# Layer-0 pair products of a DLRM tower (CIN) made for three tiles at once

## The reference, cut to what matters

```
prev = x
for k in range(3):
    z = einsum('bmd,bhd->bdmh', x, prev).reshape(b, 16, m * h)
    t = einsum('bdc,co->bdo', z, ws[k]) + bs[k]      # ws[0]: 39*39 x 128, ws[1], ws[2]: 128*39 x 128
    t = transpose(t, (0, 2, 1))
    t = t / sqrt(sum(t * t, axis=(-2, -1)))          # one norm per example
    logit.append(t); prev = t
features = sum(concatenate(logit, axis=1), axis=-1)  # then a small 400-512-256-1 network
```

## Time and profile before

| | |
|---|---|
| median of three runs | 1061.17 us |
| the profiled execution | 1062.48 us |
| its span, first to last instruction | 1060.8 us |
| TensorE (PE) busy | 97% |
| VectorE (DVE) busy | 93% |
| GpSimd (POOL) busy | 82% |
| ScalarE (ACT) busy | 75% |
| granted TensorE clock | 1.000 of full speed in the mean |

### The profile page before, as it was taken

How to read it: one execution, slowest core, us unless ns; L and a number is a source line. 1 busy time by engine, 2 the same in 40 slices (tenths; PEclk the granted TensorE clock), 3 DMA queues, 4 the chain that set the end, 5 groups by cost and what they waited for, 6 DMA issues and landing times.

```text
span 1060.8 us, 17970 instructions
## 1 busy us (share of the span) xinstructions
PE 1028.2 (97%) x4320; PEld 782.4 (74%) x4320; DVE 983.6 (93%) x3344; ACT 791.3 (75%) x2655; POOL 865.9 (82%) x729
## 2 busy tenths in 40 slices
PE   2999999999999999999999999999999999999998
PEld 0477777878777787877778787777878777788884
DVE  2589999999999999999999999999999999999993
ACT  3476877868788786868778687777868778788872
POOL 6777988889898888988888898888889888577770
PEclk9999999999999999999999999999999999999999
DMA  5650030302303030120303012030301203000000
GB/s 188 129 143 12 3 88 3 89 2 52 96 4 88 3 87 4 21 71 2 89 3 87 5 28 64 3 89 2 85 7 17 74 3 89 1 1 1 2 1 1
DMA packets 75892, 46.10 MB, mean 43 GB/s; under 512 B 55689, under 2 KB 58633, under 8 KB 75658
## 3 DMA queue, kind: packets, MB, share of 16 engines
q1 hardware_dynamic: 68487, 38.59, 15.2%
q10 hardware_dynamic: 2179, 5.07, 1.4%
q0 software_dynamic: 5120, 1.29, 1.4%
HBM read 42.99 MB, written 1.94 MB: 42 GB/s over the span
## 4 chain that ended last, share of the span: by engine, by line
PE 48%; POOL 19%; DVE 18%; issue 9%; ACT 5%; DMA 1%; POOLq 0%; DVEq 0%; SPq 0%; ACTq 0%
POOL sums L432 14%; DVE sums L946 12%; PE acc L778 8%; PE bank_d L722 7%; PE bank_d L723 6%; PE bank_d L724 6%; PE bank_a L724 6%; PE bank_a L722 6%; PE bank_a L723 6%; POOL gathered L415 5%; ACT scaled L560 4%; DVE bank_d L946 2%; DVE sums L965 1%; ACT sums L560 1%; PE turned L799 1%
## 5 line engine op out<-in xcount | busy, mean ns | idle before, releaser
L432 POOL TENSOR_TENSOR sums<-sums,scaled 128x512 f32<-128x512 f32 (+1 forms) x512 | 645.1, 1262 | 133.4 <-ACT scaled L560 97.4
L946 DVE SCALAR_TENSOR_TENSOR sums<-bank_d,x_col,sums 128x128 f32<-128x128 f32 x2304 | 654.2, 339 | 29.3 <-PE bank_d L724 20.2
L560 ACT ACTIVATE scaled<-bank_a,x_col 128x128 f32<-128x128 f32 x1920 | 551.5, 385 | 139.8 <-PE bank_a L724 132.7
L722 PE MATMUL bank_d<-w_hi,prev_lo 128*128 128x512 f32 x640 | 288.0, 450 | 6.2 <-DVE sums L965 4.7
L722 PE MATMUL bank_a<-w_hi,prev_lo 128*128 128x512 f32 (+1 forms) x640 | 263.9, 412 | 2.6 <-issue 1.3
L724 PE MATMUL bank_d<-w_hi,prev_hi 128*128 128x512 f32 x640 | 252.5, 394 | 0.0
L723 PE MATMUL bank_d<-w_lo,prev_hi 128*128 128x512 f32 x640 | 252.1, 394 | 0.0
L724 PE MATMUL bank_a<-w_hi,prev_hi 128*128 128x512 f32 (+1 forms) x640 | 245.3, 383 | 0.0
L723 PE MATMUL bank_a<-w_lo,prev_hi 128*128 128x512 f32 (+1 forms) x640 | 245.1, 383 | 0.0
L560 ACT ACTIVATE sums<-bank_a,x_col 128x128 f32<-128x128 f32 x512 | 146.1, 369 | 76.8 <-PE bank_a L724 75.9
L415 POOL DMA_INDIRECT gathered<-in_table,idx x160 | 177.2, 1108 | 28.5 <-issue 18.3
(11 more groups left out here) (84 smaller groups left out, 528.2 us busy)
## 6 DMA issues: line engine op xcount, KB each, us to landing
x_pairs<-x_scratch SPq DMA_DIRECT2D x135, 156.0 KB
x_pairs<-x_scratch SPq DMA_DIRECT2D x96, 78.0 KB
gathered<-in_table,idx POOLq DMA_INDIRECT x160
x_sq<-x_scratch SPq DMA_DIRECT2D x32, 64.0 KB
x_pairs<-x_scratch SPq DMA_DIRECT2D x92, 22.0 KB
x_scratch<-gathered SPq DMA_DIRECT2D x16, 72.0 KB
w_raw<-in_w ACTq DMA_DIRECT2D x1, 1024.0 KB, 5.1
w_raw<-in_w ACTq DMA_DIRECT2D x1, 896.0 KB
```

The source lines that it names most:

```text
L432: nc.gpsimd.tensor_tensor(out=sums[:, n % SUMS, 0:w, :], in0=sums[:, n % SUMS, 0:w, :], in1=scaled[:, a - 1, 0:w, :], op=ALU.add).then_inc ...
L560: op = nc.scalar.activation(to[:, i, :], bank_a[at % A_RING][:, i * UNITS:(i + 1) * UNITS], ACT.Copy, scale=x_of(c, q, a * PER_BANK + i))
L722: nc.tensor.matmul(to, lo, w_h, start=True, stop=False)
L946: nc.vector.scalar_tensor_tensor(out=taken(n, u) if u in LEFT else total, in0=taken(n, u), scalar=x_of(c, q, A_FIELDS + u), in1=total, op0 ...
```

## The change

The groups become [0, 1, 2], [3, 4, 5] and [6]. The extra pairs move from tiles 0, 1, 2, 3 to tiles 0, 1, 3, 4, so that each group has one copy of `x_rep`; the third tile of a group gets a third load into partitions 117 to 127 whose products meet no weights (its matmul has 117 rows). The products of a chunk then come after field 8 of the last step of the iteration before, after field 8 of step 1 and after field 2 of step 2. The matmuls of tiles 0 to 2 go to places 1, 4 and 7 of step 0, tile 3 to place 9 of step 1, tiles 4 and 5 to places 1 and 3 of step 2, and the squares stay at place 8 of step 2. `turn_x` moves to field 9 of step 2. Chunk 0 is made tile by tile throughout, with a semaphore of its own for the tiles within a group.

```diff
--- before.py
+++ after.py
@@ -27,10 +27,11 @@
 PAIR_TILES = len(PAIR_OFFSETS) // PER_TILE
 PAIR_ROWS = PER_TILE * FIELDS
 EXTRA = 128 - PAIR_ROWS
-EXTRA_PAIRS = [(0, 0, 1, FIELDS - 1), (2, 2 * EXTRA, 2 * EXTRA + 1, 2 * EXTRA - 1)]
+EXTRA_PAIRS = [(0, 0, 1, FIELDS - 1), (3, 2 * EXTRA, 2 * EXTRA + 1, 2 * EXTRA - 1)]
 SQUARES = PAIR_TILES
-PAIR_GROUPS = [[0, 1], [2, 3], [4, 5], [6]]
+PAIR_GROUPS = [[0, 1, 2], [3, 4, 5], [6]]
 NP = len(PAIR_GROUPS)
+WITH_EXTRA = [first + n for first, _, *partners in EXTRA_PAIRS for n in range(len(partners))]
 
 PICKED = 3
 SCRATCH_FIELDS = FIELDS + 5 * SLOT_FIELDS
@@ -124,11 +125,15 @@
         _made = []
         _summed = {(0, 0): [0, 1], (0, 2): [2, 3], (0, 4): [4, 5], (0, 6): [6]}
     else:
-        _first = (step_at(_it, 0), 2) if _it == 1 else (step_at(_it - 1, 7), 12)
-        _made = [_first, (step_at(_it, 0), 12), (step_at(_it, 1), 12 if _it > 1 else 17), (step_at(_it, 2), 5)]
-        _summed = {(step_at(_it, 0), 5): [0], (step_at(_it, 0), 8): [1], (step_at(_it, 1), 1): [2],
-                   (step_at(_it, 1), 4): [3], (step_at(_it, 2), 1): [4], (step_at(_it, 2), 4): [5],
-                   (step_at(_it, 2), 8): [6]}
+        _i = [step_at(_it, q) for q in range(3)]
+        if _it == 1:
+            _made = [(_i[0], 2), (_i[1], 4), (_i[2], 2)]
+            _summed = {(_i[0], 5): [0], (_i[0], 7): [1], (_i[0], 9): [2]}
+        else:
+            _last = step_at(_it - 1, 7)
+            _made = [(_last, 8), (_i[1], 8), (_i[2], 2)]
+            _summed = {(_i[0], 1): [0], (_i[0], 4): [1], (_i[0], 7): [2]}
+        _summed.update({(_i[1], 9): [3], (_i[2], 1): [4], (_i[2], 3): [5], (_i[2], 8): [6]})
     if _it:
         SQUARES_AT[step_at(_it, 1), 3] = _c
     PAIRS_AT.update({at: (_c, p) for p, at in enumerate(_made)})
@@ -138,7 +143,7 @@
 
 SQ = 32
 OVER = FIELDS - SQ
-TURNS_AT = {((0, 12) if _c == 1 else (step_at(_c - 1, 1), 8)): _c for _c in range(1, CHUNKS)}
+TURNS_AT = {((0, 12) if _c == 1 else (step_at(_c - 1, 2), 9)): _c for _c in range(1, CHUNKS)}
 
 
 W_LOADS = {1: [(0, 16), (16, 28), (28, 39)], 2: [(0, 14), (14, 27), (27, 39)]}
@@ -277,6 +282,7 @@
         turns_made = sem("turns_made")
         picked = sem("picked")
         pairs_made = sem("pairs_made")
+        first_pairs_made = sem("first_pairs_made")
         pairs_summed = sem("pairs_summed")
         x_sq_loaded = sem("x_sq_loaded")
         x_col_made = sem("x_col_made")
@@ -316,9 +322,11 @@
         y_done = sem("y_done")
         y_stored = sem("y_stored")
 
-        PAIR_LOADS = [2 * PER_TILE + 3, 2 * PER_TILE + 3, PER_TILE, 0]
-
-        NOT_LOADED = [PER_TILE + 2, 1, 0, 0]
+        PAIR_LOADS = [2 * PER_TILE + 4, 2 * PER_TILE + 4, 0]
+
+        NOT_LOADED = [PER_TILE + 3, 0, 0]
+
+        FIRST_SINGLY = [i for tiles in PAIR_GROUPS for i in tiles[:-1]]
         R_STEPS = 4
         TOP_LOADS = 2 * 3 + 2
 
@@ -358,11 +366,11 @@
                 for kk in range(PER_TILE):
                     load_rows(queue, c, p, x_rot[kk * FIELDS:(kk + 1) * FIELDS, tiles[0]:tiles[0] + len(tiles), :],
                               PAIR_OFFSETS[PER_TILE * tiles[0] + kk], [[ROWS, FIELDS], [PER_TILE * ROWS, len(tiles)]])
-            if p < 2:
-                tile, _, *partners = EXTRA_PAIRS[p]
-                for i, partner in enumerate(partners):
-                    if tile + i in tiles:
-                        load_rows(queue, c, p, x_rot[PAIR_ROWS:128, tile + i, :], partner, [[2 * ROWS, EXTRA]])
+            tile, _, *partners = EXTRA_PAIRS[p]
+
+            for i, partner in enumerate(partners + partners[:1]):
+                if tile + i in tiles:
+                    load_rows(queue, c, p, x_rot[PAIR_ROWS:128, tile + i, :], partner, [[2 * ROWS, EXTRA]])
 
         def load_squares(queue, c):
 
@@ -504,8 +512,7 @@
                 if c:
                     sp.wait_ge(pairs_made, c * NP)
                 for p in range(NP - 1):
-                    if p < 2:
-                        load_reps(sp, c, p)
+                    load_reps(sp, c, p)
                     if c:
                         load_partners(sp, c, p)
                 if c:
@@ -769,9 +776,11 @@
                 group = [p for p in range(NP) if tile in PAIR_GROUPS[p]][0]
                 if tile == 0 and c:
                     pe.wait_ge(biased, FINISH_NO[0, c - 1] + 1)
-                if tile == PAIR_GROUPS[group][0]:
+                if c == 0 and tile in FIRST_SINGLY:
+                    pe.wait_ge(first_pairs_made, FIRST_SINGLY.index(tile) + 1)
+                elif c == 0 or tile == PAIR_GROUPS[group][0]:
                     pe.wait_ge(pairs_made, c * NP + group + 1)
-                rows = 128 if tile <= EXTRA_PAIRS[-1][0] + 1 else PAIR_ROWS
+                rows = 128 if tile in WITH_EXTRA else PAIR_ROWS
                 if tile == SQUARES:
                     nc.tensor.matmul(acc0[:, :], w0s[:, :], z0s[:, :], start=False, stop=True).then_inc(pairs_summed, 1)
                 else:
@@ -790,7 +799,8 @@
 
             def pick(tile):
 
-                nc.tensor.matmul(bank_d[tile][:, :], turns[:, tile, :], x_rep[0:FIELDS, :],
+                rows = 128 if tile in WITH_EXTRA else PAIR_ROWS
+                nc.tensor.matmul(bank_d[tile][0:rows, :], turns[:, tile, 0:rows], x_rep[0:FIELDS, :],
                                  start=True, stop=True).then_inc(picked, 1)
 
             def keep_busy(count):
@@ -805,7 +815,7 @@
             keep_busy(3)
             pe.wait_ge(scratch_stored, 48)
             keep_busy(4)
-            pe.wait_ge(turns_made, 2 * PICKED)
+            pe.wait_ge(turns_made, PICKED + sum(i in WITH_EXTRA for i in range(PICKED)))
             pe.wait_ge(pairs_loaded[0], pairs_landed(0, 0))
             for tile in range(PICKED):
                 pick(tile)
@@ -902,18 +912,20 @@
                 dve.wait_ge(pairs_loaded[p], pairs_landed(c, p))
                 if c and p == 0:
                     dve.wait_ge(pairs_summed, c)
-                rows = 128 if p < 2 else PAIR_ROWS
-                if c == 0 and p < 2:
+                if c == 0:
+
                     for i in tiles:
                         if i < PICKED:
                             dve.wait_ge(picked, i + 1)
-                        mult = nc.vector.tensor_tensor(out=z0[:, i, :], in0=bank_d[i][:, :] if i < PICKED else x_rot[:, i, :],
-                                                       in1=x_reps[p][:, :], op=ALU.mult)
-                    mult.then_inc(pairs_made, 1)
+                        rows = 128 if i in WITH_EXTRA else PAIR_ROWS
+                        mult = nc.vector.tensor_tensor(out=z0[0:rows, i, :],
+                                                       in0=bank_d[i][0:rows, :] if i < PICKED else x_rot[0:rows, i, :],
+                                                       in1=x_reps[p][0:rows, :], op=ALU.mult)
+                        mult.then_inc(first_pairs_made if i in FIRST_SINGLY else pairs_made, 1)
                     return
-                nc.vector.tensor_tensor(out=z0[0:rows, tiles[0]:tiles[0] + count, :],
-                                        in0=x_reps[min(p, 1)][0:rows, :].unsqueeze(1).to_broadcast([rows, count, ROWS]),
-                                        in1=x_rot[0:rows, tiles[0]:tiles[0] + count, :],
+                nc.vector.tensor_tensor(out=z0[:, tiles[0]:tiles[0] + count, :],
+                                        in0=x_reps[p].unsqueeze(1).to_broadcast([128, count, ROWS]),
+                                        in1=x_rot[:, tiles[0]:tiles[0] + count, :],
                                         op=ALU.mult).then_inc(pairs_made, 1)
 
             def turn_x(c):
```

## The result

The changed kernel takes 1079.33 us (median of four runs: 1072.35, 1079.32, 1079.34, 1081.21), the kernel before 1062.62 us on the same occasion (median of four). The ratio is 1.0154, interval 1.0128 to 1.0181: slower by 1.5%, 16.7 us. The forecast was 1070, the range 1054 to 1079: the sign was right, the size 9 us short, and the result is 0.3 us above the range. The profiled execution is the one of 1081.21 us, 18.7 us above that of before.

A forecast was written before the change was run, and what follows sets the result against it. TensorE bounds the kernel, waiting in places for VectorE, whose products wait for GpSimd. 1062.48 + 9.1 - 0.3 = 1071.3 us profiled; the median of runs, 1.31 us less, was forecast at 1070, range 1054 to 1079.

The forecast's parts named there:

- The duration of a product: On VectorE: 1.62 us for three tiles (1536 columns), counted from the end of the GpSimd instruction it waits for.
- A: Product of tiles 0 to 2, after field 8 of the previous iteration's last step; TensorE loses 1.04 us.
- B: Product of tiles 3 to 5, step 1; waits behind GpSimd's add, TensorE loses 0.59 us before tile 3's matmul.
- Product A's place: Last step: asks at 520.14, inside `prev_lo` (519.74 to 521.04); first bank of step 0 starts at 523.50 instead of 522.56.
- The old loss: Before the change, TensorE loses about 0.93 us an iteration to VectorE's lateness, in steps 0 and 2.
- The sum for an iteration: Steady iterations: 1.04 + 0.59 - 0.93 = +0.70 us, times 13 = 9.1 us.
- B hidden: Rival, step 1: the second product starts ahead of GpSimd's add and costs nothing; +1.4 us, 1062; chance 0.24.
- both idle: Rival: both products find GpSimd idle; -8.7 us over 13 iterations, 1052; chance 0.16, nearly idle included.
- A passed over: Rival: GpSimd's next add goes ahead of the first product, which ends 1.24 us later; +16 us, 1086; chance 0.10.
- What costs nothing: Loads (landing hidden by eight microseconds), `x_rot`, `turn_x` and 128 partitions put at nothing; the opening and first iteration near it.
- chunk 0: Opening: tile 0 may start earlier, 0 to 0.3 us; tiles 3 to 5 wait for loads, -0.3 to +0.7; taken -0.3.
- Iteration 1: There and for chunk 1, waits of half a microsecond change places: 0, within 1 us.

The follow-up runs named there:

- the second experiment: Changed kernel with the second product back after field 12 of step 1, matmuls of tiles 3 to 5 at places 1, 3, 5 of step 2: 1070.51 us, 1.0082.
- The filling: Changed kernel with six instead of four filling matmuls (results unused, they keep TensorE busy) before the opening's picks: 1073.53 us, ratio 1.0107.

## Why the prediction was right in part and short in size

- *The duration of a product.* Right: A 2.51 us (2.52 forecast), ending 1.62 us after `prev_lo`, and B ending 1.62 us after the add. In the changed kernel all 28 products of chunks 2 to 15 ask while GpSimd is in an add or in `prev_lo`, and end 1.61 or 1.62 us after it: 1.05 ns a column, and nothing before. It does not hold for products that ask in a gather (see the last section).
- *Product A's place.* Right: 0.40 us into `prev_lo`; it costs 1.03 us for a forecast 1.04. Putting the product back behind field 12 gives 0.51 us for an iteration and not all of it, since step 0 then waits for the product at place 1 and at the third bank.
- *Product B.* Right: it waits behind the add, and TensorE before tile 3's matmul; it costs 0.60 us for a forecast 0.59. B asked 0.17 us inside the add; the margin had been given as 0.18.
- *The old loss.* Given as 0.93 us, it is 1.00: the last step and step 0 before are 16.40 us against 15.54 without a wait, steps 1 and 2 17.63 against 17.49. (The "four fields after field 12" of the prediction are three, fields 13 to 15; the time given for their end is theirs.)
- *The sum for an iteration.* 1.03 + 0.60 - 1.00 = 0.63, and 0.64 measured, for a forecast 0.70; times 13, 8.3 us for 9.1.
- *The rivals.* B hidden is refuted by B's length (2.73) and by the second experiment; both idle by A's 2.51; A passed over too: A ends 1.62 us after `prev_lo`, with the next add stretched by 1.28 us (three adds in 5.18 us instead of 3.90).
- *"What costs nothing".* This step failed, in two terms. The larger was chunk 0: I took -0.3 from -0.3 to +0.7 and it was +5.3 us. The passes "without a gap" of the earlier trace rows were seen, but not what stood before them: with the larger first transfers `x_rep` lands a microsecond later, TensorE idles 1.9 us before the picks, and runs most of the next ten microseconds at 1.2 GHz. The filling removes 4.8 us of it in the changed kernel, and the loads alone bring it to the old one (3.9 us by the ratio). The other was the loads, put at nothing: "eight microseconds hide its landing" was read from the kernel before in a steady iteration. In the changed kernel a steady cover is 6.5 us, which is enough, and in iteration 3, where eight other loads stand ahead in the queue, it is 5.2 us for a landing of 7.5. The wait of 2.26 us costs 2.4 us, the half clock behind it 1.4, and moving those eight loads gives 3.78 back.
- *Iteration 1.* It is 0.9 us longer where 0 within 1 us was given; the bound held. With the matmuls of tiles 0 to 2 at places 7 and 9 of step 0 and 1 of step 1 it takes 63.55 us, as before; which of their places costs the time no run shows.

With the measured terms the sum is 1062.48 + 8.3 + 5.3 + 3.8 + 0.9 = 1080.8, against 1081.21.

So the steady part was right in its mechanism and nearly in its size, and over half of the 18.7 us came from what had been put at nothing.

Left open: why the clock of the filling matmuls rises at 24.06 us in one execution and at 27.32 in another (7.8 to 9.3 us for the same fourteen), and why some idle stretches are followed by the lower clock and others not. Where the kernel before goes into the lower clock is not known either, since its profile shows none; filling cured it at no net gain.

## What to carry to other kernels

Merging instructions saves starts, but it makes the wait of whoever needs the first part of the result longer: what decides is whether the longer instruction fits the slack at its place, so try the place before the size. Here the place alone gave 1.0%; the size gave 0.30 us an iteration at the old places and lost 0.28 us in step 0. Without any wait for VectorE an iteration would take 61.25 us (an estimate: 62.89 less 1.63, 62.25 less 1.00 and 61.66 less 0.42 give 61.24 to 61.26), so the best kernel here, at 61.38, has little left to win from it. Look for the once-only stretches (opening, a queue with an extra batch of loads) and price them by their own rows: a cover read in a steady iteration says nothing of them. And price an idle gap of TensorE with and without a lower clock behind it: the same 3.1 us of idle cost 3.8 us in one execution and 2.4 in another.

## What the runs showed of the hardware

- TensorE's clock after an idle stretch. In the opening, 1.7 to 2.6 us of idle before the picks were followed by a mean granted clock of 0.50 to 0.54 from 32 to 42 us in five profiles and of 0.66 in a sixth (the first product at 12, 2.11 us idle); 0.27, 0.61 and 0.98 us by 0.83 or 0.84; 0.29 us or less in the other five by 1.00. In iterations 3 and 4, 3.17 us of idle were followed by 0.54 for 3.3 us, and 2.04 us (the loads split) by 0.63, but 3.13 us (more filling) and 2.02 us (the second product at 12) by 1.00. So the length of the idle stretch alone doesn't tell what the clock does.
- A gather of GpSimd behind a product of 1536 columns took 2.30 us, against 0.96 alone and 1.77 behind 1024 columns: it is held up by VectorE's instruction, by more the longer that is. The Trainium skill ("SBUF — State Buffer", "Who interferes with whom") infers the opposite for a gather's descriptors; the measurements decide.
- A waiting product got its turn behind `prev_lo` although GpSimd's next add was there at once, in every iteration. Behind a gather followed at once by an add it had been passed over. It isn't always so: with the products in steps 0 and 1, one asks at 350.64 us, 0.44 us into a gather, and takes 1.74 us, as if GpSimd were idle. What makes the difference no run shows.
